# Normalising inside the attention, and a product with Wo by token tiles that begins in the last quad

## The reference, cut to what matters

```python
def attn(x, Wq, Wk, Wv, Wo):            # x: (2, 2048, 512), 16 heads of 32
    q, k, v = (x @ Wq), (x @ Wk), (x @ Wv)          # each reshaped to (B, T, 16, 32)
    scores = einsum('bthd,bshd->bhts', q, k) * tril(ones((T, T)))
    attn = softmax(scores / T ** 0.5, axis=-1)      # masked scores are 0, not -inf
    out = einsum('bhts,bshd->bthd', attn, v).reshape(B, T, 512)
    return out @ Wo
xn = layernorm(x)
s = attn(xn, Wq, Wk, Wv, Wo)
g = silu(ffn(xn))                        # layernorm with gamma and beta, ternary weight, bias
return x + s * g
```

## Time and profile before

| | |
|---|---|
| median of 3 runs | 1746.27 us (1740.81 to 1749.38) |
| the profiled execution | 1746.13 us, its span 1744.4 us |
| PE busy | 1606.6 us (92%) |
| DVE busy | 1110.0 us (64%) |
| POOL busy | 872.4 us (50%) |
| ACT busy | 784.4 us (45%) |
| mean granted clock of PE | 0.945 |

### The profile page before, as it was taken

The page is one execution under the profiler, slowest core; times in us unless marked ns, Lnnn a source line. Parts: engine busy times, 40 slices in busy tenths (PEclk is TensorE's granted clock), DMA queues, the critical chain, the costliest instruction groups (busy, mean ns, idle before and its releaser), DMA issues.

```text
span 1744.4 us, 24965 instructions
## 1 busy us (share of the span) xinstructions
PE 1606.6 (92%) x9026; PEld 943.8 (54%) x9026; DVE 1110.0 (64%) x1824; ACT 784.4 (45%) x1611; POOL 872.4 (50%) x725
## 2 busy tenths in 40 slices
PE   5899999995999999999999999999999999889877
PEld 4787777774544444444445444444444444433665
DVE  7556666642886676777676676777667667710566
ACT  4322222321015555565556555655555556567211
POOL 0000000003016677677676767767667767777541
PEclk9999999998559999999999999999999999999988
DMA  5455566446920045035115304503503500131898
GB/s 181 136 179 168 187 194 193 145 164 167 221 76 26 20 86 135 20 74 132 39 34 121 90 20 91 135 20 79 135 20 85 133 22 19 53 107 31 258 331 290
DMA packets 109977, 201.38 MB, mean 115 GB/s; under 512 B 14368, under 2 KB 32288, under 8 KB 108832
## 3 DMA queue, kind: packets, MB, share of 16 engines
q1 hardware_dynamic: 98768, 177.79, 37.1%
q10 hardware_dynamic: 11088, 22.02, 3.8%
HBM read 123.22 MB, written 76.28 MB: 114 GB/s over the span
## 4 chain that ended last, share of the span: by engine, by line
PE 73%; DVE 13%; DMA 4%; issue 4%; POOL 2%; ACT 2%; SPq 1%; ACTq 0%; POOLq 0%; DVEq 0%
PE psS L1250 16%; PE psO L1273 15%; PE psM L1222 12%; PE psP L1162 10%; DVE mx L1015 6%; PE psL L1279 5%; PE psP L1175 5%; PE psP L1186 3%; DMA gr<-gate 3%; PE psT L1117 2%; PE psL L1288 2%; PE psM L1225 2%; DVE mneg L1032 2%; POOL acc L715 2%; ACT Pb L834 1%
## 5 line engine op out<-in xcount | busy, mean ns | idle before, releaser
L1015 DVE TENSOR_REDUCE mx<-psM 128x1 f32<-128x512 f32 (+3 forms) x1061 | 658.4, 676 | 328.2 <-PE psM L1222 186.5
L834 ACT ACTIVATE Pb<-psS 128x512 f32<-128x512 f32 (+3 forms) x1101 | 514.3, 528 | 394.9 <-PE psS L1250 372.0
L715 POOL TENSOR_TENSOR acc<-acc,Pb 128x1024 f32<-128x1024 f32 (+2 forms) x308 | 597.4, 1968 | 142.9 <-PE psO L1273 101.5
L1250 PE MATMUL psS<-Qs,Ks 97*128 97x512 f32 (+1 forms) x1223 | 489.4, 420 | 12.0 <-ACT Pb L834 7.7
L1222 PE MATMUL psM<-Ks,Qs 96*128 96x512 f32 (+3 forms) x1218 | 440.4, 396 | 54.3 <-DVE mx L1015 32.6
L1250 PEld LDWEIGHTS psS<-Qs,Ks 97*128 97x128 f32 x1223 | 233.0, 195 | 269.7 <-issue 125.2
L1222 PEld LDWEIGHTS psM<-Ks,Qs 96*128 96x128 f32 x1218 | 236.3, 199 | 107.9 <-DVE mx L1015 60.2
L1273 PE MATMUL psO<-Pb,Vs 128*32 128x512 f32 (+3 forms) x2304 | 275.4, 549 | 6.1 <-POOL Pb L698 6.1
L698 POOL TENSOR_SCALAR_AFFINE_SELECT Pb<-Pb 128x256 f32<-128x256 f32 x240 | 94.9, 406 | 165.9 <-ACT Pb L834 163.7
L661 POOL TENSOR_TENSOR rstd<-ve,mhalf 128x4 f32<-128x4 f32 x16 | 16.1, 1009 | 321.6 <-DVE ve L923 321.6
L1279 PE MATMUL psL<-Pb,ones 128*32 128x512 f32 (+3 forms) x1072 | 130.5, 556 | 0.0
(11 more groups left out here) (111 smaller groups left out, 1726.7 us busy)
## 6 DMA issues: line engine op xcount, KB each, us to landing
Qs<-q_hi SPq DMA_DIRECT2D x32, 512.0 KB, 13.0
Ks<-k_hi SPq DMA_DIRECT2D x32, 512.0 KB, 10.9
xt<-in_L_attn_x SPq DMA_DIRECT2D x8, 1024.0 KB, 6.1
q_hi<-st_hi SPq DMA_DIRECT2D x32, 256.0 KB, 3.2
q_lo<-st_lo SPq DMA_DIRECT2D x32, 256.0 KB, 3.3
k_hi<-st_hi SPq DMA_DIRECT2D x32, 256.0 KB, 4.0
k_lo<-st_lo SPq DMA_DIRECT2D x32, 256.0 KB, 4.3
v_quad<-vs SPq DMA_DIRECT2D x32, 256.0 KB, 3.3
```

The source lines that it names most:

```text
L715: g.tensor_tensor(to[:, :, o:], to[:, :, o:], Pb[s % RING][:, heads, o:], ALU.add).then_inc(sum_done, 1)
L834: a.activation(weights(s, h)[:, o:], score_bank(s * HQ + h, last)[:, o:], ACT.Exp, scale=SCALE).then_inc(exp_done, 1)
L1015: v.tensor_reduce(flat[:, heads, slots], all_banks[max_bank(n)][:, 0:ns * w].rearrange("p (a b c) -> p a b c", a=nh, c=w), AX.X, ALU.max). ...
L1250: t.matmul(score_bank(n, last)[:, o:], Ks[par][0:MROW + 1, h, j * P:(j + 1) * P], Qs[par][0:MROW + 1, h, c * CW + o:(c + 1) * CW], start=T ...
```

## The change

1. The division moves into the attention. `denominators` leaves the row sums in E on all 32 rows of a head; DVE now inverts E in place, in eight pieces of 64 columns, two per step over the second and third group after the chunk's end (`late`), and then multiplies cum by it (`quotients`). SP stores the normalised heads; the denominators no longer leave the core, and the broadcast loads, POOL's products and ACT's casts are gone.
2. The side work of the chunks moves to groups 0, 5, 8, 14 (`chunk_work`), since the buffers come free later.
3. The product with Wo goes by tiles of 128 tokens (`unit`, 12 products each, 32 units). The first batch's 16 units are placed in the last quad, in the steps `UNIT_STEP` = 12, 14, 16, 17, 19, 21, 23, 24, 26, 28, 30, 31, 33, 35, 37, 38. They use two of the three psM banks, so that the wide scores of the last quad have four banks instead of six. DVE makes both parts of the heads (`heads_parts`, the low one in place).
4. The weights' parts are made in step 9 of the last quad instead of at group 2.
5. The first half of the first quad is loaded head by head (24 loads instead of 6), and the maxima wait for single heads; PE waits for 4 constants instead of 7.

```diff
+def chunk_work(c):
+    return (0, 5, 8, 14)[c]
...
+        wide_banks = [psM[2][:]] + [bank[:] for bank in psS]
...
             def store_chunk(qn, c):
-                sp.wait_ge(ost_done, START + qn * NCH + c + 1).then_inc(sp_waited, 1)
+                sp.wait_ge(nrm_done, START + qn * NCH + c + 1).then_inc(sp_waited, 1)
                 sp.dma_start(num_t[bass.ds(qn * P, P), cols], cum[i][:]).then_inc(ost_out[i], 16)
-                sp.wait_ge(lst_done, START + qn * NCH + c + 1).then_inc(sp_waited, 1)
-                sp.dma_start(l_rows[bass.ds(qn * HQ, HQ), cols], E[i][::DH, :]).then_inc(lst_out[i], 16)
...
+            for h in range(HQ):
+                for g, (qa, ka) in enumerate(((q_hi, k_hi), (q_lo, k_hi), (q_hi, k_lo))):
+                    rows, cols = slice(g * DH, (g + 1) * DH), slice(0, T // 2)
+                    sp.dma_start(Qs[0][rows, h, cols].bitcast(F32), qa[h * DH:(h + 1) * DH, cols]).then_inc(kq_first[h], 16)
+                    sp.dma_start(Ks[0][rows, h, cols].bitcast(F32), ka[h * DH:(h + 1) * DH, cols]).then_inc(kq_first[h], 16)
...
             def quad(qn, par, more, follows):
                 if not more:
                     sp.wait_ge(pv_done, START + (NQUAD - 1) * NSTEP)
                     sp.dma_start(wo_s[:], w_o).then_inc(wo_in, 16)
+                    for n in range(2):
+                        load_heads(n)
+                    for u in range(DRING):
+                        load_unit(u)
                 if follows:
                     if more:
                         sp.wait_ge(pv_done, START + qn * NSTEP)
                         load_half(qn + 1, 1 - par, 1)
                         load_values(qn + 1, 1 - par)
+                    store_chunk(qn - 1, NCH - 1)
+                    load_chunk(qn, 1)
+                store_maxima(qn, 1)
                 store_chunk(qn, 0)
...
+            def store_unit(u):
+                i, ahead = unit_at(u), u + DRING - 1
+                sp.wait_ge(oo_done, u + 1)
+                sp.dma_start(out_t[u], xr[i][:]).then_inc(oo_out[i], 16)
+                if u >= 1 and ahead < RINGED:
+                    sp.wait_ge(oo_out[(u - 1) % DRING], ((u - 1) // DRING + 1) * 16)
+                    load_unit(ahead)
+                if u >= NT and u + 2 * DRING < NU:
+                    load_unit(u + 2 * DRING)
+                if u % CT == CT - 1 and u // CT + 2 < NCHUNK - 2:
+                    load_heads(u // CT + 2)
...
+            def reciprocals(qn, c, pieces):
+                i, k = c % 2, qn * NCH + c
+                dve.wait_ge(lst_done, START + k + 1)
+                for z in pieces:
+                    part = slice(z * PIECE, (z + 1) * PIECE)
+                    v.reciprocal(E[i][:, part], E[i][:, part]).then_inc(rcp_done, 1)
+
+            def quotients(qn, c):
+                i, k = c % 2, qn * NCH + c
+                dve.wait_ge(ost_done, START + k + 1)
+                dve.wait_ge(rcp_done, START + (k + 1) * NPIECE)
+                v.tensor_tensor(cum[i][:], cum[i][:], E[i][:], ALU.mult).then_inc(nrm_done, 1)
+
+            def heads_parts(n, ks):
+                whole = heads_at(n)
+                dve.wait_ge(ac_in[n % 2], (n // 2 + 1) * 16)
+                if n >= 2:
+                    dve.wait_ge(D_full, START + (n - 1) * CT)
+                for k in ks:
+                    v.tensor_copy(ah[n % 2][:, k, :], whole[:, k, :]).then_inc(ah_done, 1)
+                    dve.wait_ge(ah_done, n * KT + k + 1)
+                    v.tensor_tensor(whole[:, k, :].bitcast(F32R), whole[:, k, :], ah[n % 2][:, k, :].bitcast(F32),
+                                    ALU.subtract).then_inc(al_done, 1)
+
+            def gated(u):
+                i = unit_at(u)
+                dve.wait_ge(xg_in[i], (u // DRING + 1) * 32 if u < RINGED else 32)
+                dve.wait_ge(D_full, START + u + 1)
+                v.tensor_tensor(gr[i][:], psM[u % 2][:], gr[i][:], ALU.mult).then_inc(sg_done, 1)
+                dve.wait_ge(sg_done, START + u + 1)
+                v.tensor_tensor(xr[i][:], gr[i][:], xr[i][:], ALU.add).then_inc(oo_done, 1)
+                if NT <= u < NT + CT:
+                    if u < NT + 2:
+                        heads_parts(NCH + 1, [u - NT + 2])
+                    else:
+                        half = u - NT - 2
+                        reciprocals(NQUAD - 1, NCH - 1, range(half * NPIECE // 2, (half + 1) * NPIECE // 2))
+                elif u + CT < NU:
+                    heads_parts(u // CT + 1, ([0, 1], [2], [3], [])[u % CT])
...
+            def unit(u):
+                n, rows = u // CT, slice(u % CT * P, (u % CT + 1) * P)
+                if u < 2:
+                    pe.wait_ge(mrow_done, START + 4 * NQUAD)
+                    pe.wait_ge(wo_done, 2)
+                else:
+                    pe.wait_ge(sg_done, START + u - 1)
+                pe.wait_ge(al_done, START + (n + 1) * KT)
+                for k in range(KT):
+                    for a, (w, xx) in enumerate(((wo_h, ah[n % 2][:]), (wo_l, ah[n % 2][:]), (wo_h, heads_at(n)[:].bitcast(F32R)))):
+                        ins = t.matmul(psM[u % 2][:], xx[:, k, rows], w[:, k, :], start=(k == 0 and a == 0), stop=(k == KT - 1 and a == 2))
+                ins.then_inc(D_full, 1)
...
                     else:
                         run(None, None, s)
+                    if not more and s in UNIT_STEP:
+                        unit(UNIT_STEP.index(s))
                     values(s)
```

More of the change, by code:

```diff
@@ L161 @@
 NUP = sum(qn < 0 for qn, _ in ENTRY)
+NPIECE = 8
+PIECE = CW // NPIECE
+NU = B * NT
+DRING = 4
+RINGED = NT + DRING
+NXG = DRING + NU - RINGED
+PREP_STEP = 10
+UNIT_STEP = [12 + 7 * n + at for n in range(NCH) for at in (0, 2, 4, 5)]
+def chunk_work(c):
+    return (0, 5, 8, 14)[c]
 def max_bank(n):
@@ L594, in quad @@
                         load_values(qn + 1, 1 - par)
+                    store_chunk(qn - 1, NCH - 1)
+                    load_chunk(qn, 1)
+                store_maxima(qn, 1)
                 store_chunk(qn, 0)
-                store_maxima(qn, 1)
                 load_chunk(qn, 2)
-                if not more:
-                    reciprocals(0)
-                    for i in range(2):
-                        sp.wait_ge(ost_out[i], START + NQ * NCH // 2 * 16)
-                        sp.dma_start(ac[i][:], numerators(0, i)).then_inc(ac_in[i], 16)
                 store_chunk(qn, 1)
@@ L1053, in quad, with late @@
+            def late(qn, gr):
+                for c in range(NCH):
+                    at = FIRST[(c + 1) % NCH]
+                    if gr - at in (1, 2) and (c + 1 < NCH or qn > 0):
+                        return (qn if c + 1 < NCH else qn - 1, c), gr - at - 1
+                return None
             def quad(qn, par, more, follows):
                 for gr, (c, j) in enumerate(GROUPS):
-                    if j == 0 and (c > 0 or follows):
-                        numerators(*((qn, c - 1) if c else (qn - 1, NCH - 1)))
+                    ended = ((qn, c - 1) if c else (qn - 1, NCH - 1)) if j == 0 and (c > 0 or follows) else None
+                    if ended:
+                        numerators(*ended)
@@ L1213, in max_scores @@
                     Q, K, (segs, _, _) = Qs[m % 2], Ks[m % 2], MAXB[rest[0]]
[L1214 to L1215 removed]
+                    if m == 0 and rest[0] < NLOW:
+                        for h in range(segs[-1][0] + 1):
+                            pe.wait_ge(kq_first[h], 96)
+                    elif rest[0] == 0:
+                        pe.wait_ge(kq_low[m % 2], (m + 1) // 2 * 96)
                     if rest[0] == NLOW:
```

263 lines of the change are left out of this document (84 added, 179 removed).

## The result

The changed kernel takes 1778.93 us (median of 4 runs, 1774.21 to 1791.45) against 1747.77 for the kernel before in the same runs: 1.0198 times, 95% interval 1.0173 to 1.0224. The forecast was 1742 us, no change, in a range of 1711 to 1772: the kernel came out slower, and outside the range. The profiled execution has a span of 1780.3 us, 35.9 above that of before.

The account below looks back on a forecast made before the run. PE and DVE were taken to bound the quads, with 0.36 us to spare in a step, and DMA to be 93% busy at the close. 1744.4 - 8.5 + 36 + 34 - 65.6 = 1740.3, plus 1.7: 1742 us, range 1711 to 1772.

Parts of the forecast that it names:

- start of the attention: First loads: head-by-head loading brings the first reduction near 430 us instead of 440.35; -8.5 us, bounds -4 and -11.
- seven quads: Quads with maxima: reciprocals, quotients and moved chunk work cost 5.2 us per quad, +36 in all, bounds 15 and 70.
- last quad: Last quad: 16 added units cost +46 us, stalls that go -16.6, some stalls come; sum +34, bounds 25 to 50.
- closing stage: Product with Wo at the end: 16 units left, 60 us instead of 125.6; -65.6, bounds -74 and -55.
- The clock's toll: PE's slow products behind chunk 1's stall after step 17: already paid in the kernel before, so nothing added.
- chunk 2's quotient: Steps 26 to 29 of a quad: the quotient stops PE by 1.5 us.
- chunk 1's with the row maxima: Step 17 of a quad: last piece and quotient come on top of the row maxima's stall, 0.48 + 1.5 = 2.0 us.
- the chunk work: Chunk 1's work moved from group 3 to 5: DVE's numerator waits for POOL, PE loses 1.1 us a quad, ends 0 and 3.
- the lock rival: Quads: SBUF lock makes each quotient wait a whole GpSimd add at three places; +33 us over seven quads, 1775 us; chance 0.22.
- The piece and the quotient: DVE in the quads: a 64-column reciprocal piece takes 0.48 us to the next start, a quotient 1.5 us (0.69 to 3.05).
- The cheap rival: Quads: reciprocals cost little, quotient of 0.69 us fits PE's small gaps; seven quads cost 2 us each, 1715 us; chance 0.24.
- the case that the prediction kept for its upper bound: Last quad from step 7: each two-input DVE operation of the units waits for a GpSimd add; upper bound 50 us.

Follow-up runs that it names:

- the run of the store order: Changed kernel, but in the last quad SP stores and reloads chunk 1's buffers after the stores of units 0 to 3: 1781.8 us, 1.0196 times the kernel before.
- fastest kernel: Changed kernel with row maxima in two reductions, last-quad store of chunk 1 behind the fourth unit, seven quads' quotients of chunks 0 to 2 one group later: 1681.4 us.

## Why the prediction was wrong

Terms as predicted and as measured, in the profiled spans:

| term | predicted | measured |
|---|---|---|
| start of the attention (512.7 to 503.2) | -8.5 | -9.5 |
| seven quads | +36 | +66.6 |
| last quad | +34 | +43.8 |
| closing stage | -65.6 | -65.0 |
| sum | -4.1 | +35.9 |

**The start** was right. Loading by single heads was not slower: the first reduction begins at 428.1 us (430 forecast), the second half lands at 452.6 (454), and from there the reductions run without a gap from 453.57 to 500.31.

**The quads** carry 31 of the 40 us, and what failed there is a term put at nothing. The prediction says of chunk 1's stall: "The clock's toll is paid before too ..., so I add nothing", and for the stalls of the other places its sum has no such term at all. PE's wait for maxima rose from 25.6 to 62.9 us, by 37.3, where 36 were forecast; in the quad shown the stalls sum to 8.9 us against 3.7 before, +5.2, the forecast to the tenth. (By place it was less exact, and some luck is in the sum: chunk 2's quotient 2.7 for 1.5; chunk 1's with the row maxima 1.3 more than before for 2.0; chunks 3 and 0 0.1 for 0.6; the chunk work 1.1 for 1.1.) What was set at nothing is PE's work at half clock: seven quads have 37.2 us more idle time (31.4 + 5.8) and 29.4 more busy time (19.5 + 9.9), together the 66.6.

The run without division parts the two causes. Per quad, over the six: the moved chunk work and SP's order added 1.4 us of idle time (forecast 1.1) and 1.8 of busy time (forecast nothing); the division added 3.9 of idle time (forecast 1.5 + 2.0 + 0.6 = 4.1) and 1.5 of busy time (nothing). The wait was sized rightly in both, the toll in neither. How the toll splits between the two is rough, since the same code differs by 2 us a quad between executions. That there is one is not: the six quads of the kernel before had 812.3 us of busy time, and 810.8 in the run with the first load alone; those of the changed kernel had 831.7, and 844.1 in the run of the store order.

That the busy time is the clock's can be worked out from the traces. Over the six quads PE worked 34.1 us at half clock before and 64.2 in the changed kernel; half of the difference is 15.0 of the 19.5 us, and the other 4.4 are not explained by the clock. In all sixteen profiles, PE's busy time over six quads less half of what it worked at half clock comes to 791 to 801 us, while the busy time itself goes from 800 to 844. In the first quad some 6 of the 9.9 us come from a low clock that lasts to 531 us instead of to 528, in a quad that began 9.5 us earlier; the run with the other store order had its full clock back at 520 with the same code, so this part is one execution's.

The toll is no fixed price per stall. With the same stalls it was 12 us apart in two executions, and with the same idle time of some 18 us it was 20 us apart between many short stalls and six of 1.7 to 2.6 us.

The quads came out at 148.7 us for the 145 forecast. None of the three signs that the prediction named for being wrong came true: quads of 142 us, quotients with a median near 3, a closing stage above 70 us. The range also was narrower than its parts: its upper end of 1772 leaves out the lock rival's own time, 1775, which had a chance of 0.22, and the quads' own upper bound of 70, which alone gives 1776.

**The piece and the quotient** were sized nearly rightly (0.46 us from start to start of pieces for 0.48, a mean of 1.70 us over the seven quads for 1.5), and their cover too: pieces alone are hidden. But no quotient takes 1.5: chunk 1's, priced so, takes 0.69, and chunk 0's 2.34 are hidden, as forecast. The lock rival had the right sign and nearly the right time (1775), but by luck: it wanted the quotient to wait a whole add at three places a quad, while chunk 1's and chunk 3's do not (0.69 and 0.82), and the time it had for these waits was spent at half clock. The cheap rival's claim that DVE has room is right for the pieces and wrong for both together.

**Not seen** was that the row maxima's own 4.5 us are the same wait for GpSimd. The prediction read `mmax` at 2185 ns and took it as a price for the quotient; it didn't ask what it costs where it stood. Removing it is worth 31 to 35 us in the kernel before.

**The last quad.** PE's busy time rose by 47.3 us, where the forecast was 42.3 (46 for the units less 3.7 for slow products behind stalls that go); which part of the units took the other 5 was not looked into. Its idle time was to fall from 14.7 to 6.5 (stalls of 12.9 go, 4.7 come), and fell to 11.1: the stalls at the weights and at the selection are gone as said, but PE waited 3.9 us for a denominator's addition queued behind head parts that GpSimd held up (the case that the prediction kept for its upper bound), 2.4 for head parts themselves, and 2.6 for the gated product behind SP's late loads. That SP's stores of outputs and loads of units stand behind the store of a normalised chunk was not in the sum. In the fastest kernel, with the store behind the fourth unit, the last quad takes 153.9 us, the 154 of the forecast; with the same order it took 155.4 to 163.6 in the other kernels.

**The closing stage** was right as a sum, 61.4 us for 60. Its parts were less so: DVE waits 7.05 us for heads at its beginning where 5 were said, PE stands 5.0 for DVE's gated product behind them where unit 18 was to come 2.5 late, and 1.2 to 1.4 three times more. (The 330 GB/s of its DMA estimate are 305 in the earlier trace rows; that estimate stood off the chain.)

## What to carry to other kernels

Where PE has tenths of a microsecond to spare in a step, what an addition costs depends on what else falls in that step: spread single small pieces, and put no second thing behind them. A small VectorE operation with two SBUF inputs, or a `tensor_scalar`, beside a GpSimd that adds without pause is no small operation; make it a reduction, where it can be one, before anything is added to that engine. Count a stall of PE with the work behind it at half clock, and when a store waits for a later result, read what its queue holds behind it.

## What the runs showed of the hardware

In the changed kernel VectorE inverted 64 columns in 0.54 us and was never held up in 256 pieces (0.49 to 0.55), while operations with two SBUF inputs between them were (`cum<-cum,E` 0.68 to 2.83); `cum<-psO,cum`, of the same size with one input in PSUM, took 0.63 to 0.69 in all 32 cases. An operation on 128x32 took from 0.17 to 4.59 us, by what GpSimd did, and a reduction of 160 or 192 columns to 32 took 0.32 to 0.34. The granted clock fell to 0.5 at stalls of PE, those of 1.1 to 2.7 us among them, and its toll over six quads (busy time over the 800 us at clock 1.00) was between 0 and 44 us for idle times of 8 to 60. In two executions of the same six quads with the same idle time it was 12 us apart.
